# A graph layer with a mixture-of-experts layer behind it: where VectorE's branch closes, when the second group is turned, and the order of the last tiles

## The reference

```
x = x + gnn(layernorm(x))        # h = x @ W; out = segment_sum(h[src]*norm, dst) + b; prelu
x = x + ffn(layernorm(x)[None])
ffn: logits = mean over all nodes of x @ Wr + br      # one routing for all nodes
     routing_weights = softmax(logits), scaled by capacity, softmax again
     top 2 of 8 experts, their weights softmaxed again
     out = sum over both of w * (gelu(x @ W1[e] + b1[e]) @ W2[e] + b2[e])
     layernorm(out + x) * gamma + beta
```

## Time and profile before

| | |
|---|---|
| median of 3 runs | 1074.32 us (1073.18 to 1074.93) |
| the profiled execution | 1075.31 us |
| its span | 1073.8 us, 20081 instructions |
| TensorE busy | 1048.2 us, 98% |
| TensorE's weight loads | 892.4 us, 83% |
| VectorE busy | 815.8 us, 76% |
| ScalarE busy | 683.0 us, 64% |
| GpSimd busy | 518.9 us, 48% |
| DMA | 156.70 MB, mean 146 GB/s |

### The profile page before, as it was taken

The page is one execution under the profiler, slowest core; times in us unless marked ns, Lnnn a source line. Parts: engine busy times, 40 slices in busy tenths (PEclk is TensorE's granted clock), DMA queues, the critical chain, the costliest instruction groups (busy, mean ns, idle before and its releaser), DMA issues.

```text
span 1073.8 us, 20081 instructions
## 1 busy us (share of the span) xinstructions
PE 1048.2 (98%) x6264; PEld 892.4 (83%) x6267; DVE 815.8 (76%) x1947; ACT 683.0 (64%) x1511; POOL 518.9 (48%) x520
## 2 busy tenths in 40 slices
PE   6999999999999999999999999999899999999996
PEld 5787888888888888888888888888689999999995
DVE  6897777868686867776777777866477878878786
ACT  5794565767666676666666766675386474656551
POOL 4102566677767776777677767771201111111111
PEclk9999999999999999999999999999899999999998
DMA  9067455566766676666667666664321111111101
GB/s 291 24 247 269 129 161 159 162 193 186 205 181 193 186 203 181 190 195 190 194 178 202 189 195 181 199 183 140 133 76 45 45 44 44 44 49 39 49 30 34
DMA packets 72547, 156.70 MB, mean 146 GB/s; under 512 B 11556, under 2 KB 38062, under 8 KB 72462
## 3 DMA queue, kind: packets, MB, share of 16 engines
q0 software_dynamic: 34896, 114.40, 37.0%
q1 hardware_dynamic: 37566, 41.22, 11.9%
HBM read 129.92 MB, written 25.67 MB: 145 GB/s over the span
## 4 chain that ended last, share of the span: by engine, by line
PE 92%; DVE 2%; ACT 2%; issue 1%; DMA 1%; ACTq 0%; SPq 0%; DVEq 0%; POOLq 0%; POOL 0%
PE banks L1869 40%; PE banks L1846 14%; PE banks L1983 11%; PE banks L1887 9%; PE banks L1996 8%; PE banks L1998 4%; PE banks L1728 3%; PE banks L1718 1%; PE banks L1823 1%; ACT gh L1659 1%; DMA xs<-in_x 1%; ACT gf L1661 1%; DVE hot_src L923 0%; PE banks L1857 0%; DVE hot_key L940 0%
## 5 line engine op out<-in xcount | busy, mean ns | idle before, releaser
L751 POOL DMA_INDIRECT row<-h_table,lists x385 | 436.0, 1133 | 215.8 <-issue 132.4
L1869 PE MATMUL banks<-tab,adj 128*128 128x512 f32 x1862 | 453.1, 393 | 1.3 <-ACT adj L1594 1.3
L1869 PEld LDWEIGHTS banks<-tab,adj 128*128 128x128 f32 x1862 | 348.0, 188 | 78.7 <-DVE tab L1044 1.4
L1589 ACT CAST adj<-banks 128x784 fp32r<-128x784 f32 x296 | 226.4, 817 | 216.5 <-PE banks L1846 216.5
L1156 DVE TENSOR_TENSOR hot_src<-iota_src,turned 128x1536 bf16<-128x1536 bf16 x152 | 146.3, 963 | 121.1 <-PE banks L1846 120.4
L1164 DVE TENSOR_TENSOR hot_key<-iota_key,turned 128x588 bf16<-128x588 bf16 (+1 forms) x456 | 199.5, 491 | 0.0
L1846 PEld LDWEIGHTS banks<-hot_key,hot_src 128*128 128x128 bf16 x1776 | 148.3, 145 | 39.3 <-issue 36.3
L1846 PE MATMUL banks<-hot_key,hot_src 128*128 128x147 bf16 (+1 forms) x1776 | 174.8, 247 | 0.6 <-ACT adj L1589 0.6
L1996 PE MATMUL banks<-W2s,gh 128*128 128x512 f32 x392 | 139.0, 396 | 0.6 <-DVE pre L1419 0.6
L1659 ACT ACTIVATE gh<-banks,b1e 128x384 fp32r<-128x384 f32 (+1 forms) x136 | 79.6, 585 | 87.3 <-PE banks L1983 87.2
L1606 ACT ACTIVATE hot_row<-iota,own_dst 128x128 fp32r<-128x128 f32 x385 | 127.2, 404 | 0.0
(11 more groups left out here) (230 smaller groups left out, 1160.6 us busy)
## 6 DMA issues: line engine op xcount, KB each, us to landing
h_table<-tab SPq DMA_DIRECT2D x5, 2048.0 KB, 8.5
xin<-in_x SPq DMA_DIRECT2D x49, 128.0 KB, 4.2
x_dram<-x SPq DMA_DIRECT2D x49, 128.0 KB, 2.7
row<-h_table,lists POOLq DMA_INDIRECT x385, 3.8
x1f<-x_dram POOLq DMA_DIRECT2D x16, 384.0 KB, 3.8
out<-res SPq DMA_DIRECT2D x48, 128.0 KB, 1.7
W1a<-in_W POOLq DMA_DIRECT2D x8, 512.0 KB, 6.0
xs<-in_x SPq DMA_DIRECT2D x2, 1536.0 KB, 14.8
```

The lines of the kernel that those rows point to most:

```text
L751: g.indirect_dma_start(out=row[:, u, :].bitcast(F32), out_offset=None, in_=h_table, in_offset=bass.IndirectOffsetOnAxis(ap=lists[:, m % 2, ...
L1589: s.copy(adj[k][:, :].rearrange("p (q n) -> p q n", n=P)[:, :, at:at + 2 * GN].rearrange("p q (b n) -> p q b n", b=2), bank_pairs[j][:, :, ...
L1869: last = mm(acc[k][:, :], adj[k][:, q * P:(q + 1) * P], tab[:, q, :], start=(at == 0), stop=(at == T - 1), skip_group_check=True)
```

## The change

Three things, in three places.

1. VectorE: the `If` branch ends behind the loop over the one-hots. The sums of the last two blocks and the shifts stand in a second `If(is_dense(dve))` without an `Else`, behind the general code.
2. TensorE: b1's transpose and the turn of the second group (`turn_z(1, 1, GT)`) move from behind the branch into it, directly behind the logits; both versions get them. The fillers there go from 8 and 4 to 5 and none.
3. The last tiles: the sums of the last tile (tile 48) come on VectorE between the two steps of tile 47, and TensorE puts the high and the low weights of the last tile into the same 256 columns, so that VectorE has one sum less for it.

```diff
-    WARM = (9, 8, 4)
+    WARM = (9, 5)
...
                 for b in range(1, ND):
                     rows_of(b)
-                x1_norm(T - 3, (T - 3) % 2)
-                x1_sum(T - 2, acc[1 - LAST])
-                x1_stats(T - 2, (T - 2) % 2, 0)
-                add_loop(ND - 1)
-                x1_norm(T - 2, (T - 2) % 2)
-                shifts(0, T - 1, mean[:, 0:T - 1])
-                shift_total()
-                x1_sum(T - 1, acc[LAST])
-                x1_stats(T - 1, (T - 1) % 2, 0)
-                dve.wait_ge(sd2_made, (T - 1) * 2 + 1)
-                v.reciprocal(rstd[:, T - 1:T], sd[:, 0:1]).then_inc(epi, 1)
-                shifts(T - 1, T, mvb[:, 0:1])
             with dve.Else():
...
+            with dve.If(is_dense(dve)):
+                x1_norm(T - 3, (T - 3) % 2)
+                x1_sum(T - 2, acc[1 - LAST])
...
+                shifts(T - 1, T, mvb[:, 0:1])
...
-            def out_stats(g, k, m):
+            def out_stats(g, k, m, halves=2):
...
-                v.tensor_tensor(pre[:, m, :], y[:, 0:D], zb[:, k, m, :], ALU.add).then_inc(norm, 1)
-                hold(dve, norm, e + 1)
-                v.tensor_tensor(pre[:, m, :], y[:, D:2 * D], pre[:, m, :], ALU.add).then_inc(norm, 1)
+                v.tensor_tensor(pre[:, m, :], y[:, 0:D], zb[:, k, m, :], ALU.add).then_inc(norm, 3 - halves)
+                if halves == 2:
+                    hold(dve, norm, e + 1)
+                    v.tensor_tensor(pre[:, m, :], y[:, D:2 * D], pre[:, m, :], ALU.add).then_inc(norm, 1)
...
-            output(NG - 1, 1, GT)
-            output(NG, 0, 1)
+            out_stats(NG - 1, 1, 0)
+            for m in range(1, GT):
+                out_stats(NG - 1, 1, m)
+                out_end(NG - 1, 1, m - 1)
+            out_centre(NG - 1, 1, GT - 1)
+            out_stats(NG, 0, 0, halves=1)
+            out_scale(NG - 1, 1, GT - 1)
+            out_end(NG, 0, 0)
...
+            def last_turns():
+
+                pe.wait_ge(late_in, N_LATE)
+                nc.tensor.transpose(zsum[:, P:P + NX * KF], b1_rows[:, :], ident[0:NX * KF, 0:NX * KF]).then_inc(b1_turned, 1)
+                turn_z(1, 1, GT)
+
...
                 logits()
+                last_turns()
                 stay_warm(WARM[1])
...
                         mm(y[:, 0:2 * D], gh[:, k, c, m * P:(m + 1) * P], W2s[:, c // KF, c % KF, :, :].rearrange("p h d -> p (h d)"),
...
+                        else:
+                            mm(y[:, 0:D], gh[:, k, c, m * P:(m + 1) * P], W2h[:, c // KF, c % KF, :], start=(c == 0), stop=False, skip_group_check=True)
+                            mm(y[:, 0:D], gh[:, k, c, m * P:(m + 1) * P], W2l[:, c // KF, c % KF, :], start=False, stop=False, skip_group_check=True)
...
-            pe.wait_ge(late_in, N_LATE)
-            nc.tensor.transpose(zsum[:, P:P + NX * KF], b1_rows[:, :], ident[0:NX * KF, 0:NX * KF]).then_inc(b1_turned, 1)
-            turn_z(1, 1, GT)
-            stay_warm(WARM[2])
```

More of the change, by code:

```diff
@@ L1314, in _ @@
                 shifts(T - 1, T, mean[:, T - 1:T])
+            with dve.If(is_dense(dve)):
+                x1_norm(T - 3, (T - 3) % 2)
+                x1_sum(T - 2, acc[1 - LAST])
+                x1_stats(T - 2, (T - 2) % 2, 0)
+                add_loop(ND - 1)
+                x1_norm(T - 2, (T - 2) % 2)
+                shifts(0, T - 1, mean[:, 0:T - 1])
+                shift_total()
+                x1_sum(T - 1, acc[LAST])
+                x1_stats(T - 1, (T - 1) % 2, 0)
+                dve.wait_ge(sd2_made, (T - 1) * 2 + 1)
+                v.reciprocal(rstd[:, T - 1:T], sd[:, 0:1]).then_inc(epi, 1)
+                shifts(T - 1, T, mvb[:, 0:1])
             rs = [0]
@@ L1436, in out_end @@
                                        op0=ALU.mult, op1=ALU.add).then_inc(done, 1)
+            def out_end(g, k, m):
+                out_centre(g, k, m)
+                out_scale(g, k, m)
             def output(g, k, n, between=None):
@@ L1985, in hidden, with output @@
                         last.then_inc(h1_made, 1)
-            def output(g, k, n, between=None):
+            def output(g, k, n, between=None, halves=2):
                 pe.wait_ge(rt, ROUTE_END)
```

14 lines of the change are left out of this document (8 added, 6 removed).

## The result

| | before | after |
|---|---|---|
| median | 1074.26 us (9 runs, 1073.18 to 1075.65) | 1070.96 us (9 runs, 1069.52 to 1072.80) |
| ratio of after to before | | 0.9970, 95% interval 0.9960 to 0.9979 |
| the profiled execution | 1075.31 us, span 1073.8 | 1069.52 us, span 1068.0 |

3.30 us less, with 2.3 to 4.3 as the interval (0.0021 and 0.0040 of 1074.26); the forecast was 3.54 less and 1070.8 us.

What follows compares the result with a forecast made beforehand. The prediction took TensorE to bound the kernel (92% of the span), with gains only in the turn to the feed-forward part and the tail. 2.57 + 0 + 0.97 = 3.54 us off 1074.32 gave 1070.8 us, range 1069.4 to 1073.2.

Steps and rivals of the forecast that it cites:

- Edit 1's gain: VectorE's turn to the feed-forward part: without the jump on the path, zmean and the first gelu come 2.57 us earlier.
- Rival 2: VectorE's routing: the 2.8 us code-loading stall is only moved within it; time 1073.3 us, chance 0.12.
- Edit 1's cost: VectorE behind the last one-hots: jump 2.82 us, flag load and branch 1.12; x1_norm 0.63 late but swallowed, cost 0.
- Edit 2: TensorE's turn: hidden layer starts 3.6 us earlier, 1.0 us of it slack at the first gelu; extra gain 0.
- Rival 3: Hidden layer: fewer fillers keep TensorE at 1.2 GHz, deciding from 9.1 us on; with 15 us 1077.3 us; chance 0.04.
- Edit 3: Tail behind TensorE's last matmul: last scaling at 1067.18 instead of 1068.15, still waiting for SyncE; gain 0.97 us.
- Rival 1: Tail: only the deleted sum's 0.45 us is gained there, beside the turn's 2.57; time 1071.3 us, chance 0.17.
- upper bound: Tail: 1.35 us gained if GpSimd, not the wait for SyncE, released the last scaling.
- The sum: Whole kernel: 2.57 + 0 + 0.97 = 3.54 us less, giving 1070.8 us.

Runs made afterwards that it cites:

- e1: Kernel before with only VectorE's branch closed behind the last one-hots and the last sums in a second branch; 1072.65 us, ratio 0.9982.
- e4: Kernel before with VectorE's never-executed general code cut to one copy, the jump staying at its old place; 1071.65 us, ratio 0.9974.
- e9: Changed kernel with the first low_z put in one more If/Else on the same flag; one execution, no ratio; zmean 0.30 us later.
- e2: Kernel before with only TensorE's turns moved behind the logits and fillers 9 and 5; 1074.76 us, ratio 1.0001.
- e8: Changed kernel with twelve fillers instead of five ahead of TensorE's jump; ratio 0.9967.
- e12: e11 with tile 47's weights in one half of PSUM too, so one VectorE sum less; ratio 0.9977.
- e7: Changed kernel with no fillers instead of five ahead of TensorE's jump; ratio 0.9974.
- e11: Changed kernel with SyncE checking that tile 46's store has landed before issuing tile 47's store; ratio 0.9954.
- e3: Kernel before with only the last tiles reordered and the last tile's weights in one half; 1072.91 us, ratio 0.9990.
- e10: Changed kernel run once more without any edit, as reference on another chip; 1111.49 us against 1114.79, ratio 0.9976.

## Why the prediction was right

**Edit 1's gain** was right to the hundredth: `zmean` was to come 2.57 us earlier and did, released by the last shift sum, and the first gelu moved with it. e1 gives it alone, and e4 gives the same by a shorter jump at the old place, so the stall hangs on what lies between the jump and its target, not on the branch. Rival 2, a stall that is only moved, is out: in the changed kernel no gap of that kind stands behind 764. In the Trainium skill, "Advanced Engine Details and Errata", section Control Flow Timing, the 51 ns for a branch fit the branch itself (47 to 49 ns at L1124) and e4, where no gap shows, and not the 2.77 to 3.00 us of VectorE's idle time behind the jump over the long code. The rule of the Trainium skill, "Runtime: NRT & Kernel Launch", section Instruction fetch mechanics, that a taken branch to a place not loaded stalls, fits both.

**Edit 1's cost** came out at 0, as forecast, but not by the forecast's working. I had the jump cost 2.82 us at its new place too, and with 1.12 us for the flag `x1_norm` 0.63 us late. The jump costs at most 0.54 us there and the load with its branch 0.68 (0.65 in e9), 1.27 in all from the jump on, inside a gap of 3.31. So nothing was late, and the idle time had to cover a third of the 3.94 us that I gave it. The term that was mis-sized most is the jump: it does not cost the same wherever it stands. No packet of instructions falls in that stretch, which fits a target that was already loaded; why it was, no run shows. That the jump is cheap at the new place was luck: by the forecast's own prices it took the idle time to hide it.

**Edit 2** was worth 0, as forecast (e2: 1.0001), and the hidden layer came 3.48 us earlier, not 3.6. The slack is more than the 1.0 us that I gave it: e8 starts the hidden layer 1.24 us later and loses nothing at the first gelu. Rival 3 named TensorE's clock. It did not come about: in the five traces with edit 2 and five fillers on top of edit 1 (after, e9 to e12) the eighth gelu is 7.23 to 7.25 us behind the first, whether the hidden layer had 2.4 us at 0.50 or none. e7, with 4.7 us at 0.50, has 8.13. So the harm starts earlier than the 9.1 us from which rival 3 decided, and comes from the loss of the head start over ScalarE. Rival 3's working, that the clock was back after 3.8 to 5.8 us of work, rested on stretches cut too coarsely: the clock was at 0.50 from 769.9 on, ahead of the fillers, and in e4 it never fell.

**Edit 3** was forecast at 0.97 us and gave 0.96 at the last scaling, with the wait for SyncE where I had put it. Step by step: tile 47's scaling was to come 1.60 us behind its centre and came 1.70, the last scaling 2.93 and came 3.04. The 16 matmuls in place of 8 cost about 0.1 us, within the 0.24 that the forecast allowed. Rival 1, the lower bound of 0.45, is out. But the step from the last scaling to the time was wrong. The sum let the program end at a fixed distance behind the last scaling, and it ends at a fixed distance behind GpSimd's last power, 5.71 us. In the span edit 3 is therefore worth 1.38 us, which is what the forecast called its upper bound (1.35, for a last scaling released by GpSimd and not by SyncE). e11 shows it by experiment: there the last scaling comes 0.37 us earlier and the end does not move.

**The sum.** The parts inside the traces make 2.57 + 1.38 = 3.95 us; the forecast was 3.54 and the medians say 3.30, with an interval of 2.3 to 4.3 that holds both. So the time can't tell the two sums apart, and that the number fell so close to 3.54 is in part luck: the tail was counted 0.4 us too low, and the medians lie 0.65 below what the traces add up to.

**Open.** What GpSimd does in the 5.49 us from the end of its last power to the end of its DRAIN, in which no work of its own is seen. Why the moved jump finds its target loaded. Why the clock's stretch at 0.50 differs between two traces of one kernel. In the table of waits the closing barrier stands as `SPq L162 <- PEq L162`, 1.1 us before and 0.7 after; TensorE had long been done, and it is GpSimd that SyncE waits for.

## What to carry to other kernels

A gap put down to "issue" behind a jump over a long block can be code being loaded. Look for the queue of instruction packets in that stretch, make the code in between shorter, or move the jump to where the engine waits for another one anyway; then read its price at the new place from the sequencer's rows, for it need not be the same. Fillers are not to be judged at the first instruction behind them but at the stage that lives on the head start, and from more than one trace, since the clock scatters. And where a wait is removed just ahead of the program's end, look at who comes last to the closing barrier: here it is GpSimd, 5.71 us behind its last small operation, and the last store has 0.5 to 0.9 us in hand.

## What the runs showed of the hardware

A jump over VectorE's general code costs 2.77 to 3.00 us of idle time at its old place (before, e2, e3), nothing visible over a single copy's worth of code (e4), and at most 0.54 us over the long code at its new place (the changed kernel and all others with edit 1). Load, compare and branch cost VectorE 0.65 us (e9), and the branch alone 47 to 54 ns (L1124 and L1304). TensorE's jump over its long code shows no stall in e7: the wait for the weights begins 0.4 us behind the start of the branch, and the 2.68 us of "issue" are that wait. The program ends 5.71 us behind the end of GpSimd's last power in all fourteen traces, wherever the last scaling and its store lie. The granted clock fell to 0.50 in the turn in thirteen traces and not in e4. It came back before the hidden layer in e10, and in the first trace of the same kernel 2.4 us behind its start.
